# Attention values weighted from PSUM, and node outputs turned in another PSUM bank

## What is computed

```python
q = (h @ Wq + bq).reshape(n, 16, 8) * 16 ** -0.5
k = (h @ Wk + bk).reshape(n, 16, 8)
v = (h @ Wv + bv).reshape(n, 16, 8)
s = einsum('edh,edh->eh', q[row], k[col])     # one score per edge and head
m = segment_max(s, row)
p = exp(s - m[row])
z = segment_sum(p, row)
out = segment_sum(p / z[row] * v[col], row)
x = layernorm(x + out)
```

## Time and profile before

| | |
|---|---|
| median of 3 runs | 2299.91 us (2297.91 to 2305.53) |
| the profiled execution | 2304.62 us, of it span 2302.7 us |
| busy: PE, weight loads | 1626.5 us (71%), 1233.5 us (54%) |
| busy: DVE, ACT, POOL | 1501.0 us (65%), 430.7 us (19%), 1632.2 us (71%) |
| first and last start of a gather of attention | 1708.8 and 2258.2 us |

### The profile page before, as it was taken

How to read it: one execution, slowest core, us unless ns; L and a number is a source line. 1 busy time by engine, 2 the same in 40 slices (tenths; PEclk the granted TensorE clock), 3 DMA queues, 4 the chain that set the end, 5 groups by cost and what they waited for, 6 DMA issues and landing times.

```text
span 2302.7 us, 31884 instructions
## 1 busy us (share of the span) xinstructions
PE 1626.5 (71%) x8440; PEld 1233.5 (54%) x8464; DVE 1501.0 (65%) x5109; ACT 430.7 (19%) x906; POOL 1632.2 (71%) x1687
## 2 busy tenths in 40 slices
PE   4877777774676666776467666666646998888886
PEld 3555555553555554554344444444434777777775
DVE  8766676765666665765345555555666877777775
ACT  0000000002000000001211111111245444344342
POOL 7777777775777777775777777777227777777771
PEclk9999755555565666655577787787875555555555
DMA  5233233232232333233322333332334333333331
GB/s 140 56 83 85 57 84 86 56 85 57 70 84 73 96 84 112 57 85 108 102 83 84 99 91 91 99 99 84 72 116 120 110 109 111 108 108 107 108 107 33
DMA packets 148739, 207.32 MB, mean 90 GB/s; under 512 B 48280, under 2 KB 110603, under 8 KB 148320
## 3 DMA queue, kind: packets, MB, share of 16 engines
q0 software_dynamic: 60512, 138.18, 22.3%
q1 hardware_dynamic: 86898, 65.12, 9.4%
q10 hardware_dynamic: 1154, 1.99, 0.3%
HBM read 172.41 MB, written 36.04 MB: 91 GB/s over the span
## 4 chain that ended last, share of the span: by engine, by line
POOL 55%; issue 20%; PE 11%; DMA 8%; DVE 5%; ACT 1%; DVEq 0%; POOLq 0%; ACTq 0%; SPq 0%
POOL G L532 39%; POOL G L1418 17%; PE p_g L594 4%; DMA G<-in_x,idx 3%; DMA G<-h_d,idx 3%; PE p_d L605 1%; DMA kv_d<-kv_s 1%; PE p_o L625 1%; PE p_d L640 1%; PE p_w L1485 1%; DMA G<-kv_d,idx 0%; DVE work L1010 0%; DVE work L994 0%; DVE S L954 0%; PE p_o L626 0%
## 5 line engine op out<-in xcount | busy, mean ns | idle before, releaser
L532 POOL DMA_INDIRECT G<-h_d,idx x832 | 795.7, 956 | 284.4 <-issue 262.2
L594 PE MATMUL p_g<-S,G 128*128 128x96 f32 (+1 forms) x2496 | 610.4, 391 | 469.9 <-DMA G<-h_d,idx 315.9
L594 PEld LDWEIGHTS p_g<-S,G 128*128 128x128 f32 x2496 | 527.7, 293 | 673.5 <-issue 315.1
L1418 POOL DMA_INDIRECT G<-kv_d,idx x416 | 424.2, 1020 | 178.6 <-issue 177.9
L532 POOL DMA_INDIRECT G<-in_x,idx x416 | 402.5, 968 | 132.2 <-issue 118.0
L979 DVE TENSOR_SCALAR work<-iota_h,key_f 128x600 bf16<-128x600 f16 x416 | 169.0, 406 | 259.1 <-PE p_d L605 258.5
L954 DVE SCALAR_TENSOR_TENSOR S<-con,rel,shared 128x96 f32<-128x96 f32 (+1 forms) x1248 | 314.6, 292 | 0.7
L605 PE MATMUL p_d<-work 128*128 128x312 bf16 (+1 forms) x832 | 272.8, 429 | 19.9 <-DVE work L994 18.9
L972 DVE TENSOR_TENSOR agg<-agg,p_g 128x96 f32 (+1 forms) x624 | 143.0, 229 | 112.9 <-PE p_g L594 89.0
L1485 PE MATMUL p_w<-oh,PV 128*128 128x40 f32 x832 | 197.8, 413 | 0.1
L994 DVE TENSOR_TENSOR work<-work,p_d 128x312 f32 (+1 forms) x416 | 190.8, 459 | 10.7 <-issue 9.3
(11 more groups left out here) (249 smaller groups left out, 2001.1 us busy)
## 6 DMA issues: line engine op xcount, KB each, us to landing
work<-A_d SPq DMA_DIRECT2D x25, 800.0 KB, 4.5
A_d<-work SPq DMA_DIRECT2D x12, 1600.0 KB, 7.5
G<-h_d,idx POOLq DMA_INDIRECT x832, 2.5
G<-in_x,idx POOLq DMA_INDIRECT x416, 2.5
G<-kv_d,idx POOLq DMA_INDIRECT x416, 2.8
h_d<-XH SPq DMA_DIRECT2D x75, 64.0 KB
h_d<-in_x SPq DMA_DIRECT2D x2, 1600.0 KB, 7.3
QW<-q_d SPq DMA_DIRECT2D x104, 30.0 KB, 1.9
```

Source lines behind the costliest of these rows:

```text
L532: pool.indirect_dma_start(G[:, c % GRING, :], None, l.table, bass.IndirectOffsetOnAxis(ap=l.places[:, c:c + 1], axis=0)).then_inc(s_arr[g ...
L594: last = pe.matmul(p_g[:, g % PB, 0:width], G[:, c % GRING, :], S[:, c % (SRING * GR), 0:width], start=(k == 0), stop=(k == GR - 1))
L1418: pool.indirect_dma_start(G[:, c % KRING, :], None, d["kv"], bass.IndirectOffsetOnAxis(ap=idx[:, c:c + 1], axis=0)).then_inc(s_arr[c // QC ...
```

## The change

`values` takes the weights of its quarter from `p_bk` (PSUM), where PE left them, and no longer from `ps` (SBUF); it still waits for ScalarE's copy. As `p_bk` is now read by VectorE for longer, the output tiles leave it for `p_sm`, columns 264 to 399 (128 of values, 8 of normalisers), and the waits on PE follow: `rows` waits until the output tiles posted so far are divided, `weights_back` waits for all values of the batch before, `output_t` waits for fade_log. The last tile stays in `p_sT`.

```diff
-    X_COL, X_DIF, X_OUT = 256, 258, 128
+    X_COL, X_DIF, X_OUT = 256, 258, 264
...
     def p_po(t):
-        return p_bk if t < NT - 1 else p_sT
+        return p_sm if t < NT - 1 else p_sT
...
         def rows(k):
             pe.wait_ge(s_fb, k + 1)
+            if (n := posted_before(k + 1)) > 0:
+                pe.wait_ge(s_ot, n)
             pe.matmul(p_sm[0:1, 0:P], FB[:, 0, P - 1:P], ident, start=True, stop=True)
...
             pe.wait_ge(s_ex, k + 1)
             if k > 0:
                 pe.wait_ge(s_ps, k)
-            if (n := posted_before(k + 1)) > 0:
-                pe.wait_ge(s_ot, n)
+                pe.wait_ge(s_pv, 4 * k)
             pe.transpose(p_bk[:, 0:P], pT[:], ident).then_inc(s_bk, 1)
...
             if t < NT - 1:
-                pe.wait_ge(s_ps, min(POST_AT[t], KB))
+                pe.wait_ge(s_a1, min(POST_AT[t], KB) - 1)
                 if t > 0:
                     pe.wait_ge(s_ot, t)
...
             dve.tensor_tensor(PV[:, q % VRING].rearrange("p c (d h) -> p c d h", h=HEADS),
                               G[:, slot:slot + QC, D:2 * D].rearrange("p c (d h) -> p c d h", h=HEADS),
-                              bc(ps[:, k % 2, j * QC:(j + 1) * QC, :], 2, HD), ALU.mult).then_inc(s_pv, 1)
+                              bc(p_bk[:, j * QC * HEADS:(j + 1) * QC * HEADS].rearrange("p (c h) -> p c h", h=HEADS), 2, HD), ALU.mult).then_inc(s_pv, 1)
```

## The result

| | before | after |
|---|---|---|
| median | 2299.36 us (6 runs, 2296.42 to 2305.53) | 2288.51 us (6 runs, 2285.79 to 2290.07) |
| profiled execution, its span | 2304.62 us, 2302.7 us | 2288.98 us, 2287.2 us |
| first gather of attention to the end | 593.9 us | 581.2 us |
| ratio | | 0.9949, 95% interval 0.9935 to 0.9963 |

10.85 us less; forecast were 14, inside a range of 2279 to 2298 us. The span fell by 15.5 us, but 2.8 of that lie ahead of the first gather of attention (1708.8 before, 1706.0 after), where no code changed. Attention itself took 12.7 us less. In the kernel after, L1784 is L1785, L1747 is L1748, L1701 is L1702, L1681 is L1682, and `rows` is L1456.

A forecast was written before the change was run, and what follows sets the result against it. Bound by the PE, ACT, DVE chain, then from step 10 by gathers. Chain steps of 20.20 + 0.29 + 0.03 = 20.52 us put the last marker at 2249.2 against 2263.95: about 14 us gained, 2286 us, range 2279 to 2298.

The forecast's parts named there:

- The two limits: Attention's steps: the PE, ACT, DVE chain wants 20.20 us; gathers want 20.0 plus excess, setting the pace after step 10.
- Part 1's price: Values reading p_bk in PSUM instead of ps: 8 ns more an instruction, 0.03 us a step, 0.7 us over 21 steps.
- L1694's price: Upper bound for values reading PSUM, from a strided walk over 512 elements taking 1067 ns: 1.5 us a step.
- Part 1's relief: Gathers starting under values no longer held once values have one SBUF input: up to 18.5 us of POOL's time gained.
- Waits (a) and (b): On PE: weights_back waits for the previous batch's values, output_t for fade_log; both forecast to cost nothing.
- The rows wait: PE's rows waits until the step's output tile is divided: 0.29 us, counting in full in each step with an output.
- The last step: Attention's final step, where PE and ACT have no one-hots to prepare: 1 us taken off.
- the tail: Behind the last head-sums marker: 38.7 us as before, plus up to 1 us since PE no longer arrives rested.
- The collisions move: Rival, 16%, 2295 us: the phase changes and one-hots hold gathers instead, 1 us of excess every step.
- Not relieved, so 2300 us: Rival, 10%, 2300 us: G's second half being read holds gathers, not the count of SBUF inputs; POOL's pace stays.
- Slower: Rival, 5%, 2310 us: values reading 8 PSUM values 16 times over is slow, at most 1.5 us a step.

The follow-up runs named there:

- e2b: Kernel after, but output tiles in p_sT (the last in p_sm) and no new wait ahead of rows; values still from PSUM: 2282.23 us, ratio 0.9931 to before.
- e3b: As e2b, and the one-hots read the iota from spare columns of p_bk in PSUM instead of SBUF: 2282.67 us, ratio 0.9931 to before.
- e1b: Kernel after, but values read ps in SBUF again; outputs stay in p_sm with the three new waits: 2289.13 us, ratio 0.9959 to before.
- e7b: Kernel before with one edit: rows waits for the division of the output tile (s_ot): 2289.56 us, ratio 0.9959 to before.
- e6: As e2, but values read ps in SBUF: 3005.33 us, ratio 1.000, where before took 3004.28 us.
- e2: Same kernel as e2b, run on the chip where before took 2985.22 us: 2985.32 us, ratio 0.9997.
- e5b: Kernel after, but rows waits for the tile's layernorm statistics (s_bs), 0.65 us later than its division: 2996.53 us, ratio 0.9982, where before took 3004.28 us.
- e8: Kernel before, but rows waits for the first instruction of the outputs (s_z1): 2982.01 us, ratio 0.9917, where before took 3004.28 us.
- e1: Same kernel as e1b, run on the chip where before took 2985.22 us: 3003.93 us, ratio 1.0064.

## Why the prediction was right, and where not

*The two limits* (20.20 us for the chain, 21.39 where gathers set the pace): right, but the gathers lost 0.67 us a step of their lead in the first stretch, not about 1. Every kernel here that keeps its lead runs at its chain's step: 20.20 in e2b and e3b, 20.59 after, in e1b and in e7b.

*Part 1's price.* I took 8 ns more for an instruction; it takes 3 less (679 against 682). The upper end, L1694's price, did not show. Nor did the 65 ns by which an instruction on PSUM would cost more than one on SBUF by the Trainium skill ("Perfetto Trace Analysis", Optimizing Scalar/DVE Operations).

*Part 1's relief.* The mechanism is right: 44 gathers under values and none long, and with e3b the one-hots as a second case. The traces agree with the Trainium skill's rule of two SBUF inputs against a GpSimd instruction that reads SBUF ("SBUF — State Buffer", Who interferes with whom). The same section's inference that a tensor_tensor does not hold up descriptor generation does not carry over to these gathers, whose issue it lengthened from 0.95 to 1.35 us. But 18.5 us of holds are no 18.5 us of time. Without the rows wait part 1 is worth 17.6 us (before to e2b, 2299.83 to 2282.23, the move to `p_sT` included); with it, 0.6 us (2289.13 to 2288.51), less than the intervals of the two ratios, 0.9959 and 0.9949, can tell. It is luck, then, that the relief looks confirmed by the time: had values not been relieved, the same 2289 us would have come out, and only the trace tells the two apart. The step of mine that failed is here, though the sum did not depend on it: I treated the holds as a load that POOL carries whatever VectorE does. They depend on the rhythm of both. My statement that no gather under L1774 was long holds only for those that L1774 still covers some 0.1 us after their start: at 1871.80 one starts under it, values follow 0.10 us later, and it takes 1.60.

*Waits (a) and (b).* Free, as forecast; e7b, which lacks them, equals e1b, which has them.

*The rows wait.* On the chain in full, right. Its size was short: 0.39 instead of 0.29 us a step, since the matmul of rows starts 0.14 us after the division ends and I had put 0.05. The step came out at 20.59 instead of 20.52; over 20 steps that is 1.4 us, the difference between the 14 us forecast and the 12.7 of attention in the two profiles. The rest to 10.85 lies between runs: the profiled execution of before was 5.3 us above its median, that of after 0.5. What I missed is its other side: as the only edit it is a gain of 0.41%.

*The last step* took 19.4 us instead of 20.6 (I had taken 1 us off), the tail 39.1 instead of 38.7 (up to 1 added). Both right in size. My reason for the added 1 us, that PE arrives less rested, no run shows: in the tail the granted clock was 0.50 before and after.

*The rivals.* "The collisions move" had the right idea, that phase decides. Those under the one-hots did grow, from 8.2 to 9.1 us, far from its 1 us a step, and the chain covered them. In the chances I counted over half of it (2289 to 2298, centre 2295) as below 2293, where less than half of that stretch lies. "Not relieved, so 2300 us" had its premise refuted by the trace, and its time by e1b: without relief it is 2289. "Slower" fell with 679 ns.

**Open.** e6, the corner with values from SBUF and no rows wait but outputs in `p_sT`, gave no time in the regime of interest; that part 1 and not the move to `p_sT` brings e2b's gain is inferred from the steps being those of before (20.20 us) and from the holds, which e6 has and e2 lacks. e5b and e8 gave none either. Why POOL settles at 31 for two steps at 20.20 us and at 16 a step at 20.59 was seen, not derived; whether it is the length of the step that decides, or where in it the wait moves the instructions, no run separates.

**The better version** is e2b: values from PSUM, outputs in `p_sT`, no wait ahead of rows, 2282.2 us. It is clear of e1b on the same chip (2289.1) and, by its steps of 20.20 us, of after.

## What to carry to other kernels

When one engine's short instructions hold another's, sum the holds only as an upper bound: the two can fall into a common rhythm, and 2% more in one's period (20.20 to 20.59 us) took the holds from 29.5 to 18.6 us. Test a change's parts one at a time, the costs too: here the part that looked like a price brought as much alone as the whole change. And compare the pace of each engine with the step it serves before taking load off it; e3b took another 4.2 us off the gathers' busy time (400.1 in e2b, 395.9) and gained nothing, because the chain was already the floor.

## What the hardware showed that I had not expected

- A held gather ends 0.82 to 0.84 us after values or the one-hots that hold it (0.76 us after the scans L1719 and L1720), wherever in them it started. POOL and VectorE fall into fixed ratios: 31 gathers for two steps of 20.20 us before, 16 for one of 20.59 in e7b.
- It goes the other way too. Head sums, which read two SBUF tensors, take 0.29 us, but 0.31 to 0.36 in 14 of the 15 cases, over six traces, where a gather starts within 0.05 us of them. The 0.36 us in the earlier trace rows is one, and the gather is not lengthened:

```profile
1801.71 0.95 POOL L1418 DMA_INDIRECT G<-kv_d,idx  x1 [0.30 <-issue]
```
- Four one-hots back to back (1.01 us) hold a gather until the fourth has ended; of two values back to back the first alone held it in the case shown (1.35 us with a pair of 1.28).
- The kernel before took 2298 to 2300 us in three batches and 2985 and 3004 us in two others, with gather instructions of the same length; e2 kept PE, DVE and ACT busy for 1634, 1486 and 431 us there, within 1.2% of e2b's 1620, 1503 and 431. The small ratios turned over there: e1 was 1.0064 and e1b 0.9959.
